# A megakernel for attention and feed-forward: six layer norms of the first stage on GpSimd, and 64 swapped columns in its weights

## The reference

```
h  = layernorm(x)                                   # over 512 features
q  = rmsnorm(h @ Wq_a) * w_q  @ Wq_b                # rank 192, then 32 heads of 128 + 64
ckv = h @ Wkv_a ; compressed, k_pe = ckv[:64], ckv[64:]
kv = rmsnorm(compressed) * w_kv @ Wkv_b             # 32 heads of 128 + 128
q_pe, k_pe = rope(q_pe), rope(k_pe)                 # 64 wide, one k_pe for all heads
rope(v) = cat(v[0::2], v[1::2]) * cos + rotate_half(...) * sin
x  = x + layernorm(softmax(causal(q k^T * scale)) v @ Wo)
x  = x + layernorm(ffn(layernorm(x)))               # gated, low-rank terms added
```

## Time and profile before

| what | value |
|---|---|
| median of 3 runs | 588.58 us (587.62 to 589.62) |
| the profiled execution, its own time | 586.39 us |
| its span in the trace | 584.5 us |
| busy: PE / DVE / ACT / POOL | 95% / 77% / 68% / 34% of the span |
| PE busy from 13 to 46 us | 30.62 of 33.00 us |
| granted TensorE clock, mean | 0.994 |

### The profile page before, as it was taken

How to read it: one execution, slowest core, us unless ns; L and a number is a source line. 1 busy time by engine, 2 the same in 40 slices (tenths; PEclk the granted TensorE clock), 3 DMA queues, 4 the chain that set the end, 5 groups by cost and what they waited for, 6 DMA issues and landing times. The chain is left out here.

```text
span 584.5 us, 10800 instructions
## 1 busy us (share of the span) xinstructions
PE 555.9 (95%) x3246; PEld 422.1 (72%) x3246; DVE 447.6 (77%) x1203; ACT 396.4 (68%) x1173; POOL 196.1 (34%) x204
## 2 busy tenths in 40 slices
PE   4898999999999999999999999999799999988995
PEld 4676778777787787787777777776588888644564
DVE  5878787787777777877877877879678889887466
ACT  4566787887888787787878878878443553444343
POOL 2225354344444543543454454450000000045520
PEclk9999999999999999999999999999899999999998
DMA  8821213212312322231111110015570000001003
GB/s 338 316 75 50 78 58 114 85 52 87 118 51 79 92 87 78 64 114 38 52 50 39 50 46 20 21 52 185 189 298 1 1 0 1 32 7 48 2 19 126
DMA packets 21864, 46.91 MB, mean 80 GB/s; under 512 B 2864, under 2 KB 5424, under 8 KB 21552
## 3 DMA queue, kind: packets, MB, share of 16 engines
q1 hardware_dynamic: 21808, 46.23, 23.5%
HBM read 39.80 MB, written 6.42 MB: 79 GB/s over the span
## 5 line engine op out<-in xcount | busy, mean ns | idle before, releaser
L747 DVE CUSTOM_DVE_ANT_0 ss<-bank,cst 128x128 f32<-128x128 f32 (+3 forms) x256 | 125.1, 489 | 72.5 <-PE bank L1091 41.0
L468 ACT ACTIVATE pt<-bank 128x128 f32<-128x128 f32 (+3 forms) x256 | 110.1, 430 | 63.1 <-PE bank L1159 62.8
L460 ACT ACTIVATE pr<-ss,small 128x128 f32<-128x128 f32 (+3 forms) x256 | 143.1, 559 | 5.8 <-DVE small L747 4.3
L356 POOL TENSOR_TENSOR qrot<-qrot,qswp 64x512 f32<-64x512 f32 x64 | 82.0, 1282 | 116.1 <-DVE qrot L739 113.7
L1159 PE MATMUL bank<-ident,pr 128*128 128x128 f32 x640 | 113.7, 275 | 1.6 <-ACT pr L460 1.5
L1159 PEld LDWEIGHTS bank<-ident,pr 128*128 128x128 f32 x640 | 78.3, 141 | 23.6 <-ACT pr L460 6.1
L363 POOL TENSOR_TENSOR qt_lo<-qrot,qt_hi 128x384 fp32r<-128x384 f32 x64 | 64.5, 1008 | 72.6 <-ACT qt_hi L450 71.4
L1089 PE MATMUL bank<-kt_hi,qt_hi 128*128 128x256 f32 (+2 forms) x192 | 80.8, 421 | 0.3 <-DVE small L747 0.3
L1171 PE MATMUL bank<-pt,kvn 128*64 128x256 f32 (+3 forms) x512 | 75.2, 434 | 0.7 <-ACT pt L468 0.7
L1171 PEld LDWEIGHTS bank<-pt,kvn 128*64 128x64 f32 x512 | 38.8, 137 | 41.0 <-issue 28.3
L1091 PE MATMUL bank<-kt_hi,qt_lo 128*128 128x256 f32 (+2 forms) x192 | 65.0, 339 | 0.0
(11 more groups left out here) (179 smaller groups left out, 1096.4 us busy)
## 6 DMA issues: line engine op xcount, KB each, us to landing
rsb<-rinv_scratch SPq DMA_DIRECT2D x64, 128.0 KB, 2.9
sv<-sv SPq DMA_DIRECT2D x10, 576.0 KB, 4.7
sqa<-sq SPq DMA_DIRECT2D x16, 320.0 KB, 3.1
wv_raw<-wvo_scratch SPq DMA_DIRECT2D x8, 512.0 KB, 4.8
sve<-sv SPq DMA_DIRECT2D x6, 576.0 KB, 11.0
wvo_scratch<-vs SPq DMA_DIRECT2D x11, 256.0 KB, 2.2
xa<-x SPq DMA_DIRECT2D x8, 256.0 KB, 5.1
sqr<-sq SPq DMA_DIRECT2D x16, 128.0 KB, 2.3
```

Of the source, the lines that this page charges most:

```text
L356: nc.gpsimd.tensor_tensor(qrot[RKV:P, h, :], qrot[RKV:P, h, :], qswp[RKV:P, h, :], ALU.add)\
L460: nc.scalar.activation(pr[:, k % 4, 0:n], ss[:, RING[k], 0:n], ACT.Exp, bias=negmax[:, k % 8:k % 8 + 1], scale=-1.0, accum_out=rsum[:, k:k ...
L468: nc.scalar.activation(pt[:, b, h, 0:i + 1, i * P:(i + 1) * P], bank[2 + k % 2][:, 0:(i + 1) * P].rearrange("p (j q) -> p j q", q=P), ACT. ...
L747: nc.vector.tensor_tensor_reduce(out=ss[:, RING[k], 0:n], in0=bank[k % 2][:, 0:n], in1=mask[:, SEQ - n:SEQ], scale=-SCALE, scalar=3.4e38, ...
```

## The change

GpSimd, at steps t = 2 to 7, normalises tile t; VectorE keeps the tiles 0 and 1, and keeps all moments and reciprocals. `LAT` grows from 320 to 384 columns: behind the 64 key columns (evens, then odds) stand the same 64 columns with odds first. So the product leaves both the key part and its swapped form in the bank, and one VectorE product of 128 columns with `kcs` makes both terms. GpSimd adds them as before. The tile `kcs` moves to another place in SBUF.

```diff
-LAT = RQ + RKV + ROPE
+LAT = RQ + RKV + 2 * ROPE
...
-            for t in range(3, TB + 3):
+            for t in range(2, TB + 3):
+                if t < TB:
+                    pool.wait_ge(f.xn_made, t)
+                    pool.wait_ge(f.rstd_made, t + 1)
+                    nc.gpsimd.tensor_scalar(xn[:, t, :], xa[:, t, :], st1[:, t, 6:7], st1[:, t, 9:10],
+                                            ALU.subtract, ALU.mult).then_inc(f.xn_made, 1)
                 if 0 <= t - 3 < TB:
                     u = t - 3
-                    pool.wait_ge(f.krot_parts, 3 * (u + 1))
-                    nc.gpsimd.tensor_tensor(kvn[:, u, RKV:P], kra[:, u, :], krb[:, u, :], ALU.add).then_inc(f.kvn_made, 1)
+                    pool.wait_ge(f.krot_parts, u + 1)
+                    nc.gpsimd.tensor_tensor(kvn[:, u, RKV:P], krot[:, u, 0, :], krot[:, u, 1, :], ALU.add).then_inc(f.kvn_made, 1)
...
             def normalise(t):
                 dve.wait_ge(f.std_made, t + 1)
                 nc.vector.reciprocal(st1[:, t, 9:10], st1[:, t, 8:9]).then_inc(f.rstd_made, 1)
-                dve.wait_ge(f.rstd_made, t + 1)
-                nc.vector.tensor_scalar(xn[:, t, :], xa[:, t, :], st1[:, t, 6:7], st1[:, t, 9:10],
-                                        ALU.subtract, ALU.mult).then_inc(f.xn_made, 1)
+                if t < 2:
+                    dve.wait_ge(f.rstd_made, t + 1)
+                    nc.vector.tensor_scalar(xn[:, t, :], xa[:, t, :], st1[:, t, 6:7], st1[:, t, 9:10],
+                                            ALU.subtract, ALU.mult).then_inc(f.xn_made, 1)
...
-                    nc.vector.tensor_tensor(kra[:, u, :], lat[:, RQ + RKV:LAT], kcs[:, q, 0, :], ALU.mult)\
-                      .then_inc(f.krot_parts, 1)
-                    nc.vector.tensor_tensor(krb[:, u, 0:HR], lat[:, LAT - HR:LAT], kcs[:, q, 1, 0:HR], ALU.mult)\
-                      .then_inc(f.krot_parts, 1)
-                    nc.vector.tensor_tensor(krb[:, u, HR:ROPE], lat[:, RQ + RKV:LAT - HR], kcs[:, q, 1, HR:ROPE],
-                                            ALU.mult).then_inc(f.krot_parts, 1)
+                    nc.vector.tensor_tensor(krot[:, u, :, :], lat[:, RQ + RKV:LAT].rearrange("p (s n) -> p s n", s=2),
+                                            kcs[:, q, :, :], ALU.mult).then_inc(f.krot_parts, 1)
```

More of the change, by code:

```diff
@@ L35 @@
 NOPE, ROPE, VD = 128, 64, 128
-HR = ROPE // 2
-LAT = RQ + RKV + ROPE
+LAT = RQ + RKV + 2 * ROPE
 SCALE = float(NOPE + ROPE) ** -0.5
@@ L143, in build @@
     lnw = fi2.take("lnw", [P, RQ + RKV])
-    kcs = fi2.take("kcs", [P, QB, 2, ROPE])
-    kra = fir.take("kra", [P, TB, ROPE])
-    krb = fir.take("krb", [P, TB, ROPE])
+    krot = fir.take("krot", [P, TB, 2, ROPE])
     sqj = fir.take("sqj", [P, 2, RQ])
+    kcs = fir.take("kcs", [P, QB, 2, ROPE])
     st1 = fi2.take("st1", [P, TB, 16])
@@ L1426, in put @@
         return a
-    wkv_a = np.concatenate([I["attn_Wkv_a"][:, :RKV], I["attn_Wkv_a"][:, RKV:][:, evens_odds]], 1)
+    odds_evens = np.r_[1:ROPE:2, 0:ROPE:2]
+    wkv_a = np.concatenate([I["attn_Wkv_a"][:, :RKV], I["attn_Wkv_a"][:, RKV:][:, evens_odds],
+                            I["attn_Wkv_a"][:, RKV:][:, odds_evens]], 1)
     wa = np.concatenate([I["attn_Wq_a"], wkv_a], 1).reshape(DC, P, LAT).transpose(1, 0, 2)
```

## The result

The changed kernel takes 591.22 us, median of six runs (589.10 to 593.37), against 588.40 us (587.62 to 589.62) for the kernel before: a ratio of 1.0047, 95% interval 1.0029 to 1.0066. It is slower by 2.8 us (1.7 to 3.9). The forecast was 590.6 us, and slower by 2.0 us. The profiled execution took 591.32 us of its own time; before, 586.39.

The account below looks back on a forecast made before the run. TensorE was taken to bound the first stage; wider products, transfer and GpSimd's normalisation, less the wait before tile 4, made 2.14 us, less 0.11 for the rotation 2.03, giving 590.6 us. The range was 588.3 to 592.0.

Parts of the forecast that it names:

- GpSimd's instruction over 1.4 us: First stage: one of the signs named in advance that would show the prediction wrong; the normalisation was expected near 0.98 us.
- second rival: GpSimd's normalisation is much slower, 2 us each, through fetching scalars or meeting VectorE: +3.0 us, 591.6 us; chance 0.15.
- transfer, tile 0's products later: Start of the kernel: the larger `wa` lands what follows 0.34 us later, ScalarE's copies add 0.08: 0.42 us.
- rotation, one product: VectorE: one product of 128 columns takes 0.21 us in place of 0.32 for three, gaining 0.11 us.
- GpSimd's normalisation: Tiles 2 to 7: 0.98 us each on GpSimd, between bounds of 0.55 and 1.36 us.
- tile 3's transposes later: TensorE, first stage: 1.06 - 0.11 + 0.64 = 1.59 us later, at 17.87 us.
- tile 4's products later: TensorE: the 0.91 us wait for `xt_lo` goes, so the products start 1.69 - 0.91 = 0.78 us later.
- The cover of the later tiles: Later GpSimd normalisations cost nothing; tile 5 keeps 0.97 us of room, gone at about 2 us per instruction.
- the hand-over from GpSimd to TensorE: Before tile 3's transposes: 0.26 us from GpSimd's end to TensorE's start.
- The fourth rival: Attention takes up the shift, at most 1.4 us of it: +0.6 us, 589.2 us; chance 0.13.
- the first: Rival: TensorE's higher clock comes sooner, tile 0's products all run at 2.4 GHz: +0.3 us, 588.9 us; chance 0.08.
- The third: Rival: extra columns hide at 2.4 GHz because something else sets TensorE's pace: +0.0 us, 588.6 us; chance 0.10.

Follow-up runs that it names:

- `gpsimd_prices`: The changed kernel with another form of GpSimd operation in each of the tiles 2 to 7, normalisation partly left out; run once for its timeline, no time given.
- `columns_unused`: The kernel before with 64 more columns transferred, split and multiplied but read by nobody; three rotation products stay: 589.31 us, ratio 1.0024.
- `moments_late`: The kernel before with VectorE's moments taken one step later, behind `xt_lo`, from tile 4 on, and ScalarE's root moved with them: 585.79 us, ratio 0.9965.
- `after_wd_late`: The changed kernel with the down weights in feed-forward rounded by ScalarE eight steps later and split by VectorE seven steps later: 588.95 us, ratio 1.0016.
- `before_wd_late`: The kernel before with the down weights in feed-forward rounded by ScalarE eight steps later and split by VectorE seven steps later: 585.98 us, ratio 0.9967.

## Why the prediction was right, step by step

The forecast, slower by 2.0 us, held: 2.8 us (1.7 to 3.9), 591.22 us in a range of 588.3 to 592.0. The path was right too: dearer columns on the fullest engine, and GpSimd at tile 3. One price in it was wrong by a factor of two, and by the prediction's own sign (GpSimd's instruction over 1.4 us) that part had failed. The measured time lies nearer to the 591.6 us of the second rival than to the forecast's 590.6. Its terms:

| step | predicted | measured | at |
|---|---|---|---|
| 64 columns, at 2.4 GHz | 0.028 us per product | 0.027 | 15.58 to 16.10 us |
| the same in tile 0 | 0.053 us | 0.054 | 12.11 to 12.43 us |
| transfer, tile 0's products later | 0.42 us | 0.14 | 9.88 to 10.02 us |
| rotation, one product | 0.21 us | 0.19 | 15.44 to 15.63 us |
| GpSimd's normalisation | 0.98 us | 2.08 | 16.47 us |
| tile 3's transposes later | 1.59 us | 2.32 | 18.60 us |
| tile 2's products later | 1.01 us | 1.75 | 19.43 us |
| tile 4's products later | 0.78 us, no wait | 1.53, no wait | 28.59 us |
| the last transposes later | 2.0 us | 2.56 | 46.90 us |

**The mis-sized term** is GpSimd's normalisation. The prediction took 0.98 us between the bounds 0.55 and 1.36, and 2.08 lies outside. The upper bound rested on the two-input product, on the thought that one input is cheaper than two. In `gpsimd_prices` the kind of operation decides, not the number of inputs: 0.61 us for a copy, 1.04 for a two-tensor product, 1.49 for a product with one constant. The second rival had the price, about 2 us, with a total of 591.6. Its consequence was wrong, though: it let every tile wait from there on, and the full price of 1.10 us more is paid once, at tile 3.

**The cover of the later tiles** is what the prediction worked out for tile 5. It took that tile as ready at 24.35 us where the row gives 23.75 + 0.70 = 24.45, so the room was 0.1 us smaller than it says; "gone at about 2 us per instruction" came true all the same. GpSimd ends tile 5 at 27.60 us and TensorE starts on it at 27.65, 1.07 us behind the start before it where 1.01 is usual (24.16 to 25.17 before): 0.06 us of waiting. The transposes of tile 2's latents then come 0.67 us later in place of 0.49, since GpSimd's copy for them, behind the normalisation, ends at 28.07.

**Tile 3 again, by terms.** The prediction had +1.59 us. To it come +1.10 for the price and +0.13 for GpSimd's later start behind the reciprocal (0.33 in place of 0.20 us), which the prediction left out; from it go 0.28 for the transfer, 0.21 for the hand-over and 0.02 for the rotation. That makes 2.31, and 2.32 was measured.

**Two errors in the other direction.** The transfer was to bring 0.34 us, and 0.42 with ScalarE's part. In the changed kernel VectorE gets tile 1 of x at 6.48 in place of 5.73 us, but this start scatters by itself: 5.69 to 5.80 us in four narrow kernels, 6.39 and 6.56 in two, 6.33 to 6.79 in the six with 384 columns. What the larger transfer brings by itself is therefore not shown. What the later start brings is then taken back in part. In the kernel before, VectorE's normalisation of tile 1, in its timeline,

```profile
7.21 1.22 DVE L836 TENSOR_SCALAR xn<-xa,st 128x512 f32<-128x512 f32 x1
```

took 1.22 us; in the changed one it lasts 0.62 (7.95 us). So 0.60 of 0.75 us come back, and 0.14 is left. GpSimd's split of `wa` runs beside it in both (5.64 to 9.14 us, 6.34 to 10.39), so that alone does not explain the difference, and its cause is not shown. The Trainium skill, "SBUF — State Buffer", "Who interferes with whom", says that VectorE and GpSimd contend for one pair of ports under an exclusive lock. A duration that doubles in one execution (1.22 us) and not in another (0.62) is compatible with that, but no run here tests it. It was luck for the number that this gave back what the late start cost. The second is the hand-over from GpSimd to TensorE, 0.05 us (18.55 to 18.60) for the 0.26 taken.

**From tile 2 to tile 4** the prediction has two tiles of wide products against a wait of 0.91 us, -0.23 us together; measured -0.22 (1.75 to 1.53). The agreement is partly luck: from start to start the wait gave back 1.13 us, not 0.91 (25.66 to 27.06 us before, 28.32 to 28.59 after), and the 0.24 us of GpSimd at tile 5 took that up. From tile 4 to the end it has +1.25, measured +1.03.

**Behind the stage** the shift is carried on: +2.56, +2.73 behind attention, +3.01 at feed-forward. The fourth rival, attention taking up part of it, did not come. Nor did the first: tile 0's products all ran at the slow distance in the changed kernel. The third, columns hidden, is refuted by the distances and by `columns_unused`.

## What to carry to other kernels

An engine that waits at few places is not relieved by moving work at all places: find the wait, and look first whether an order of the same instructions removes it (`moments_late`: -2.1 us, with nothing added). Columns added to a product on the fullest engine are paid, less the waits that they happen to fill, whatever they spare on another; here 3.0 us more of TensorE's work made the stretch 1.72 us longer and bought 0.3. And a price on another engine is only taken from the same kind of operation there; work that leaves the queue of a fast engine must still meet the tightest of its deadlines, which sat at tile 3 here.

## What the runs showed of the hardware

- On GpSimd, 128x512 f32: copy 0.61 us; product of two tensors with a broadcast column 1.04; with one constant 1.49, one scalar of each partition 1.57; two operations with constants 1.92, with scalars 2.08. The product of two tensors is cheaper than that of a tensor and a scalar. The 2.08 us do not change with what VectorE does beside it.
- VectorE's normalisation of tile 1 beside GpSimd's split of the weights took 1.05 to 1.23 us in six of the kernels and 0.56 to 0.70 in seven, with the same operands. In feed-forward the delay fell on either side: `xf_lo` took 1.76 us in `after_wd_late` with GpSimd's product at 1.31, and 0.68 us in `before_wd_late` with GpSimd's product at 1.93, though in both kernels `xf_lo` started at 533.84 us and GpSimd's product at 533.74.
- With no edit of the transfers, the arrival of the first transfers scatters by up to 0.9 us between profiled executions. Differences of such a size at the start of a kernel are no evidence on an edit; distances behind it, here the stretch, are.
- The granted clock was below 1.00 in exactly one of the two windows of each profile, 120 us apart (0.91, once 0.83). The waits before it, 1.61 to 3.09 us with a fall in feed-forward and 0.55 to 2.62 without, do not sort the cases. In the changed kernel six products at 0.43 in place of 0.23 us cost about 1.2 us of the profile; the timed runs do not show such a difference.
